# Clearing finished stages' semaphores inside the following stage, in a two-layer graph network kernel

## The chip, the core and the metric

The kernel runs on one core of a Trainium2 chip. The core has five engines with a queue of instructions each: TensorE (PE in the rows; PEld are its weight loads), VectorE (DVE), ScalarE (ACT), GpSimd (POOL) and SyncE (SP). SyncE computes nothing here; it issues most of the transfers. Engines wait for each other by semaphores, counters that one instruction raises and another waits on. The metric is the device time of one execution in microseconds (us); lower is better.

## What is computed

There are 50,000 nodes with 64 features, and 50,000 edges sorted by `dst`. Two layers follow each other, each a layer norm with ReLU, a pass over the edges that sums into nodes, and a residual:

```python
h = relu(layernorm(x));  Wh = h @ W + b
sim = cosine(Wh[src], Wh[dst])                      # layer 0
x = x + scale * (c0 * segment_sum(base * relu(sim) * Wh[dst], src)
               + c1 * segment_sum(-base * relu(-sim) * Wh[dst], src) + c2 * Wh)
h = relu(layernorm(x))                              # layer 1
msgs = mlp(concat(h[dst], h[src]))
agg = segment_sum(msgs, dst)
x = x + mlp(concat(h, agg))
```

## The kernel before

`build` runs six stages in this order. `prepare` loads the edge lists and makes tables. `node_phase0` (tag n0) does layer norm and `Wh` in 49 blocks of 1,024 nodes. `edge_phase` of layer 0 (tag e0) goes through 98 groups of 512 edges: GpSimd gathers rows by index (L1096) and adds results to the table `x1` by index (L1111), and SyncE loads the windows of rows (L1069). `node_phase1` (n1) is the second layer norm, again 49 blocks: SyncE loads `n_x` (L671) and stores `n_h` (L666), and GpSimd also zeroes the table of sums. `edge_phase` of layer 1 (e1) has 98 groups again; TensorE multiplies, VectorE adds into that table (L882). `node_phase2` (n2) is the last MLP over 49 blocks: VectorE copies `agg_sb` beside the rows `n_hs` that SyncE loaded (L1447), TensorE turns them (L1481) and multiplies (L1490).

Each stage is one `Block` or more: every engine runs its own program, and at the Block's end each engine does a DRAIN and then all five meet at a barrier, an EVENT_SEMAPHORE record on each engine in the trace. The records of such an end carry the line of the stage's `Block`: L726 for both edge stages, L648 for n1, L80 for the block that clears. No engine begins the next stage before that barrier. Within a stage each engine's order is a software pipeline written out by `rounds_of_blocks` (L423 is its loop). In the edge stages every engine has two programs, one for graphs whose edges lie near enough together and one for others, and chooses by a value read on the chip (`both_ways`, L733); with these inputs it is the first, and each engine ends it with a jump over the code of the other.

Semaphores are counted up during a stage and have to be zero before their number is used again. The class `Semaphores` keeps a list of those that stages have made. After e0 and again after e1, `give_back` opens a Block of its own in which SyncE clears every semaphore in the list, one instruction each, while the other four engines have nothing in that Block but its barrier; then the numbers are free for the next stages. The first list has 82 semaphores (22 of `prepare`, 31 of n0, 29 of e0), the second 87 (26 of n1, 61 of e1).

At the end of n1 SyncE waits until its stores have landed (L675):

```python
rounds_of_blocks(sp, [(1 - SLOTS, store), (0, load)])
for s in range(SLOTS):
    sp.wait_ge(stored[s], 16 * (ROUNDS + (s == 0)))
```

Of the kernel before, what the change touches and what calls it, by code (L numbers as in the profile page):

```python
# [68 lines left out]
class Semaphores:  # L69
# [5 lines left out]
    def new(self, name):  # L75
        self.made.append(self.ctx.enter_context(self.nc.semaphore(name)))
        return self.made[-1]

    def give_back(self):
        with self.nc.Block() as block:  # L80
            @block.sync
            def _(sp):
                for sem in self.made:
                    sp.sem_clear(sem)
        self.ctx.close()
        self.ctx, self.made = ExitStack(), []


def began(k):

    return not isinstance(k, int) or k > 0


def count(s, k, back=0, slots=0):

    return (slots or SLOTS) * k + s + 1 - back
# [7 lines left out]
def rows_of(tab, base, r=R):  # L104

    return tab[bass.ds(base, P * r), :].rearrange("(p r) d -> p (r d)", r=r)


def build(nc, x, src, dst, edge_weight, edge_weight_n2, W, b, deg_coeff, coeff_param, scale_param,
          mW1, mb1, mW2, mb2, uW1, ub1, uW2, ub2, out):  # L110
    ctx = ExitStack()
    with ctx:
        def sb(name, shape, dt=FP32):
            return ctx.enter_context(nc.sbuf_tensor(name, shape, dt))

        def table(name, shape):
            return nc.dram_tensor(name, shape, FP32, kind="Internal").ap()


        tabs = {name: table(name, [ROWS, D]) for name in ("wh", "x1", "h1", "agg")}  # L120

        tabs["ends"] = table("ends", [2, TILES, P])
        tabs["rel"] = nc.dram_tensor("rel", [TILES, P], FP16, kind="Internal").ap()

        c = dict(
            sems=Semaphores(nc),

            gathered=[[ctx.enter_context(nc.semaphore(f"e{layer}_gathered{s}")) for s in range(ESLOTS)]
                      for layer in range(2)],
            added=[[ctx.enter_context(nc.semaphore(f"e{layer}_added{s}")) for s in range(ESLOTS)]  # L130
                   for layer in range(2)],
            ident=sb("ident", [P, P]),
            not_before=sb("not_before", [P, G * P]),
            near=sb("near", [1, 1], INT32),
            first_i=sb("first_i", [1, TILES], INT32),
            in_window=sb("in_window", [P, WK]),
            in_span=sb("in_span", [P, SPAN], FP16),
            rel_col=sb("rel_col", [P, GROUPS, G]),
            at_i=sb("at_i", [1, TILES], INT32),
            zeros=sb("zeros", [P, SPARE * D]),  # L140
            eps_ln=sb("eps_ln", [P, 1]),
            trash=sb("trash", [P, G]),
            w_blk=sb("w_blk", [P, 2 * D]),
            b_rows=sb("b_rows", [1, R, D]),
            ones_row=sb("ones_row", [1, P]),
            mw1=sb("mw1", [P, DH]), mw1_odd=sb("mw1_odd", [P, DH]), mb1_col=sb("mb1_col", [P, 1]),
            mw2=sb("mw2", [P, D]), mb2_row=sb("mb2_row", [P, D]),
            uw1=sb("uw1", [P, DH]), ub1_col=sb("ub1_col", [P, 1]),
            uw2=sb("uw2", [P, D]), ub2_row=sb("ub2_row", [P, D]),
            mix=sb("mix", [P, 3]),  # L150
            edge_f=sb("edge_f", [P, 3, GROUPS, G]),
            edge_i=sb("edge_i", [P, 2, GROUPS, G], INT32),
            bank=[ctx.enter_context(nc.psum_tensor(f"bank{i}", [P, 512], FP32)) for i in range(8)],
        )
        prepare(nc, c, tabs, src, dst, edge_weight, edge_weight_n2, W, b, deg_coeff, coeff_param,
                scale_param, mW1, mb1, mW2, mb2, uW1, ub1, uW2, ub2)
        node_phase0(nc, c, tabs, x)
        edge_phase(nc, c, tabs, layer=0)
        c["sems"].give_back()
        c["agg"] = sb("agg_sb", [P, NB * D])  # L160
        node_phase1(nc, c, tabs)
        edge_phase(nc, c, tabs, layer=1)
        c["sems"].give_back()
        node_phase2(nc, c, tabs, out)


# [262 lines left out]
def base_of(s, k):  # L429

    if isinstance(k, int) and k * SLOTS + s == BLOCKS - 1:
        return LAST_BASE
    return (k * SLOTS + s) * BLOCK


def rows(a):
    return a.rearrange("p (r d) -> p r d", d=D)
# [205 lines left out]
            rounds_of_blocks(pe, [(-3, turn), (-4, multiply)])  # L643


def node_phase1(nc, c, tabs):

    with ExitStack() as ctx:  # L648
        slots = Slots(nc, c, ctx, "n1")
        h = slots.bufs("h", [P, R * D])  # L650
        ln = LayerNorm(nc, c, slots, [rows(a[:]) for a in h])
        stored = slots.sems("stored")
        agg_clear = slots.sem("agg_clear")
        ln.h_act_ready = slots.sem("h_act_ready")
        SPLIT = R // 2 + 1
        block = ctx.enter_context(nc.Block())

        @block.sync
        def _(sp):
            def store(s, k):  # L660
                sp.wait_ge(ln.h_ready, count(s, k))
                sp.wait_ge(ln.h_act_ready, count(s, k))
                base = base_of(s, k)
                if base is LAST_BASE:
                    sp.wait_ge(stored[SLOTS - 1], 16 * k)
                sp.dma_start(rows_of(tabs["h1"], base), h[s][:]).then_inc(stored[s], 16)  # L666

            def load(s, k):
                if began(k):
                    sp.wait_ge(ln.xc_ready, count(s, k, SLOTS))  # L670
                sp.dma_start(ln.x[s][:], rows_of(tabs["x1"], base_of(s, k))).then_inc(ln.x_in[s], 16)  # L671

            rounds_of_blocks(sp, [(1 - SLOTS, store), (0, load)])
            for s in range(SLOTS):
                sp.wait_ge(stored[s], 16 * (ROUNDS + (s == 0)))  # L675

        @block.vector
        def _(dve):
            def normed(s, k):
                if began(k):  # L680
                    dve.wait_ge(stored[s], 16 * k)
                ln.dve_h_of(dve, s, k, SPLIT)

            rounds_of_blocks(dve, [(0, lambda s, k: ln.dve_total(dve, s, k)), (-3, lambda s, k: ln.dve_rstd(dve, s, k)),
                                   (0, lambda s, k: ln.dve_mean(dve, s, k)),
                                   (-2, lambda s, k: ln.dve_squares(dve, s, k)), (-3, normed)])

        @block.gpsimd
        def _(pool):
            def centre(s, k):  # L690
                pool.wait_ge(ln.mean_ready, count(s, k))
                if began(k):
                    pool.wait_ge(ln.h_ready, count(s, k, SLOTS))
                    pool.wait_ge(ln.h_act_ready, count(s, k, SLOTS))
                nc.gpsimd.tensor_tensor(rows(ln.xc[s][:]), rows(ln.x[s][:]), by_row(ln.mean[s][:]),
                                        ALU.subtract).then_inc(ln.xc_ready, 1)

            def clear(s, k):
                if isinstance(k, int) and k < 2:
                    i, part = k * SLOTS + s, NB * D // (2 * SLOTS)  # L700
                    nc.gpsimd.memset(c["agg"][:, i * part:(i + 1) * part], 0.0).then_inc(agg_clear, 1)

            rounds_of_blocks(pool, [(0, centre), (0, clear)])
            pool.wait_ge(agg_clear, 2 * SLOTS)

        @block.scalar
        def _(act):
            def normed(s, k):
                if began(k):
                    act.wait_ge(stored[s], 16 * k)  # L710
                ln.act_h(act, s, k, range(SPLIT, R))

            rounds_of_blocks(act, [(-2, lambda s, k: ln.act_std(act, s, k)), (0, lambda s, k: ln.act_square(act, s, k)),
                                   (-3, normed)])


def edge_phase(nc, c, tabs, layer):
    with ExitStack() as ctx:
        slots = Slots(nc, c, ctx, f"e{layer}")
        if layer == 0:  # L720
            near = far = EdgeBuffers(c, slots, layer)
        else:
            with ExitStack() as own:
                near = NearBuffers(c, Slots(nc, c, own, f"e{layer}"))
            far = EdgeBuffers(c, slots, layer)
        with nc.Block() as block:  # L726
            edge_programs(nc, block, c, tabs, near, far, layer)


def edge_programs(nc, block, c, tabs, near, far, layer):  # L730
    def both_ways(eng, close, apart):
        is_near = eng.value_load(c["near"][0:1, 0:1], min_val=0, max_val=1)
        with eng.If(is_near > 0):  # L733
# [5 lines left out]
    def _(sp):  # L739
        def apart():  # L740
            edge_loads(nc, sp, c, tabs, far, layer, False)
            if layer == 1:
                for s in range(ESLOTS):
# [4 lines left out]

        both_ways(sp, lambda: edge_loads(nc, sp, c, tabs, near, layer, True) if layer == 0 else near_sync(nc, sp, c, tabs, near),
                  apart)  # L750

    @block.gpsimd
    def _(pool):
# [784 lines left out]
```

## Time and profile before

| | |
|---|---|
| median of 3 runs | 2421.32 us (2419.44 to 2427.26) |
| profiled execution, device time | 2421.7 us |
| its span, first to last instruction | 2419.1 us |
| busy: PE, DVE, ACT, POOL | 1563.3, 1546.1, 864.6, 1689.1 us |
| mean granted TensorE clock | 0.684 of full speed |
| bytes moved | 273.11 MB |

The span is what the trace covers; 2.6 us of the device time lie outside it. No engine is busy over 70% of the span, because the stages have different bounds. Registers, branches, semaphore instructions and the issue of transfers are not counted as busy, so the time that SyncE spends on clearing is in no line of busy time; the queue records, whose engine name ends in q (SPq, DVEq), show it.

How the rows are read. A row of a stretch has its start and end, its length, the busy us of PE, PEld, DVE, ACT and POOL each with the number of instructions, the granted clock (1.00 is full speed), the share of the DMA engines and GB/s. A row of the timeline has start, duration, engine, line, operation and tiles, and in brackets how long the engine had been idle and who released it. A row of records has a line, an engine, an operation, its count, the least, median and greatest duration in ns, and when the first and the last began.

### The profile page before, as it was taken

Reading aid. Unit: us, or ns where it says so; the run is one execution under the profiler, and the core shown is the slowest. Engines: PE = TensorE matmul, PEld = TensorE weight load, DVE = VectorE, ACT = ScalarE, POOL = GpSimd, SP = SyncE. Lnnn points to the kernel's source line nnn. Section 1 sums busy time; section 2 is a strip of 40 time slices with the busy share of each in tenths; the row PEclk is TensorE's granted clock in tenths of the full one; section 3 lists DMA queues with packets and bytes.
Section 4 is the critical chain, followed back from the end, with each engine's and each line's share of the span. In section 5 each row is a group of like instructions: output and inputs, shape, how many; then the busy total and the mean of one; then the engine's idle time right before and its main releaser. Section 6 shows DMA issues by size and latency. Waiting matters only on the chain. (4 is left out here: it accounts for less than half of the span.)

```text
span 2419.1 us, 57388 instructions
## 1 busy us (share of the span) xinstructions
PE 1563.3 (65%) x16004; PEld 1340.3 (55%) x16004; DVE 1546.1 (64%) x5636; ACT 864.6 (36%) x3093; POOL 1689.1 (70%) x1413
## 2 busy tenths in 40 slices
PE   4886755555455454554555540005999999997998
PEld 2555645545455454554554540005999999994454
DVE  5995655555545555555555551894999999994554
ACT  3773322222222222222222221562333333333665
POOL 2775888888888888888888885746777777751322
PEclk6996555555555555555555555557999999998999
DMA  3775544444444444444444422565555555424664
GB/s 99 251 247 172 114 81 84 75 83 82 76 85 80 78 84 74 85 83 75 85 75 83 84 35 15 181 219 150 125 125 124 126 124 126 123 70 119 187 188 145
DMA packets 342562, 273.11 MB, mean 113 GB/s; under 512 B 144834, under 2 KB 273514, under 8 KB 342484
## 3 DMA queue, kind: packets, MB, share of 16 engines
q1 hardware_dynamic: 259028, 233.22, 33.3%
q0 software_dynamic: 81536, 38.61, 15.1%
q8 instruction: 33, 0.54, 0.1%
q10 hardware_dynamic: 1920, 0.37, 0.1%
q14 instruction: 45, 0.37, 0.0%
HBM read 206.69 MB, written 65.34 MB: 112 GB/s over the span
## 5 line engine op out<-in xcount | busy, mean ns | idle before, releaser
L1111 POOL DMA_INDIRECT x<-e_sums,e_to x392 | 622.7, 1588 | 126.1 <-issue 118.6
L1346 PE MATMUL bank<-e_parts,e_same 128*128 128x64 bf16 x2940 | 172.8, 241 | 579.9 <-DVE e_parts L1205 579.9
L1298 PE MATMUL bank<-e_window,e_onehot 128*128 128x64 f32 x2352 | 525.3, 422 | 16.5 <-DMA e_window<-wh 16.5
L1298 PEld LDWEIGHTS bank<-e_window,e_onehot 128*128 128x128 f32 x2352 | 511.8, 332 | 16.9 <-issue 16.8
L1096 POOL DMA_INDIRECT e_ends<-wh,e_ids x392 | 419.1, 1069 | 132.7 <-issue 101.2
L1346 PEld LDWEIGHTS bank<-e_parts,e_same 128*128 128x128 bf16 x2940 | 159.4, 129 | 595.9 <-issue 595.9
L823 POOL DMA_INDIRECT e_near_source<-h,e_near_ids x392 | 394.9, 1007 | 129.0 <-issue 90.2
L1244 ACT ACTIVATE e_sq<-e_ends 128x64 f32<-128x64 f32 x784 | 188.7, 242 | 680.0 <-DMA e_ends<-wh,e_ids 679.9
L1169 DVE SCALAR_TENSOR_TENSOR e_prod<-e_ends 128x64 f32<-128x64 f32 x392 | 65.5, 222 | 363.4 <-DMA e_ends<-wh,e_ids 363.4
L933 PE MATMUL bank<-e_near_to_edge,e_near_window 128*64 128x128 f32 x2352 | 154.5, 282 | 176.3 <-DMA e_near_window<-h 176.3
L933 PEld LDWEIGHTS bank<-e_near_to_edge,e_near_window 128*64 128x64 f32 x2352 | 130.8, 140 | 182.4 <-DVE e_near_to_edge L844 176.7
L1153 DVE SCALAR_TENSOR_TENSOR e_same<-e_owners,e_ef,not_before 128x512 bf16<-128x512 f32 (+3 forms) x392 | 193.3, 549 | 7.3 <-DVE e_ef L1145 4.6
L1415 POOL TENSOR_TENSOR n_x<-n_x,ub_row 128x512 f32<-128x512 f32 x49 | 62.2, 1270 | 183.6 <-DMA n_x<-x 183.6
L906 ACT ACTIVATE e_near_hid<-bank,mb_col 128x512 f32<-128x512 f32 x98 | 67.4, 688 | 330.6 <-PE bank L953 330.6
L882 DVE TENSOR_TENSOR agg_sb<-bank,agg_sb 128x256 f32 x392 | 162.0, 413 | 1.2 <-DVE agg_sb L882 0.6
L977 PEld LDWEIGHTS bank<-e_near_parts,e_near_to_node 128*128 128x128 bf16 x4704 | 150.3, 98 | 17.6 <-DVE e_near_to_node L851 3.9
L977 PE MATMUL bank<-e_near_parts,e_near_to_node 128*128 128x64 bf16 x4704 | 153.2, 193 | 3.6 <-DVE e_near_parts L866 2.6
L1244 ACT ACTIVATION_READ_ACCUMULATOR e_sq<-e_ends 128x1 f32 x784 | 146.1, 186 | 0.0
L1137 DVE TENSOR_SCALAR e_onehot<-e_rel,in_window 128x512 f32<-128x512 f16 x294 | 127.3, 488 | 11.5 <-DMA e_rel<-rel 11.5
L1436 ACT ACTIVATE n_hid<-bank,ub_col 128x512 f32<-128x512 f32 x98 | 103.0, 1154 | 77.9 <-PE bank L1490 77.8
L851 DVE TENSOR_SCALAR e_near_to_node<-in_span,rel_col 128x512 bf16<-128x512 f16 x392 | 127.9, 368 | 0.0
L844 DVE TENSOR_SCALAR e_near_to_edge<-e_near_rel,in_window 128x512 f32<-128x512 f16 x294 | 124.4, 475 | 4.6 <-DMA e_near_rel<-rel 4.6
(150 smaller groups left out, 2857.7 us busy)
## 6 DMA issues: line engine op xcount, KB each, us to landing
e_window<-wh SPq DMA_DIRECT2D x392, 96.0 KB
e_near_window<-h SPq DMA_DIRECT2D x392, 96.0 KB
e_owners<-ends SPq DMA_DIRECT2D x98, 256.0 KB, 3.0
n_x<-x SPq DMA_DIRECT2D x98, 256.0 KB, 3.1
n_x<-in_x_dram SPq DMA_DIRECT2D x49, 256.0 KB, 2.8
wh<-n_wh SPq DMA_DIRECT2D x49, 256.0 KB, 2.0
x<-n_x SPq DMA_DIRECT2D x49, 256.0 KB, 2.3
e_rel<-rel SPq DMA_DIRECT2D x98, 128.0 KB, 3.3
```

What stands on the lines that cost most here:

```text
L823: pool.indirect_dma_start(out=t.source[s][:, j, :], out_offset=None, in_=tabs["h1"], in_offset=bass.IndirectOffsetOnAxis(ap=t.ids[s][:, j: ...
L851: nc.vector.tensor_scalar(t.to_node[s % 2][:, j, :], c["in_span"][:], c["rel_col"][:, bass.ds(ESLOTS * k + s, 1), j:j + 1].rearrange("p a ...
L882: nc.vector.tensor_tensor(here, sums, here, ALU.add).then_inc(t.agg_ready, 1)
L933: last = nc.tensor.matmul(bank[s % 2][half:half + D, j * P:(j + 1) * P], t.window[s][:, j, w, :], t.to_edge[s % 2][:, w, j * P:(j + 1) * P ...
L977: last = nc.tensor.matmul(to[:, at:at + D], t.to_node[s % 2][:, j, b * P:(b + 1) * P], t.parts[s % 2][:, part, j, :], start=part == 0, sto ...
L1096: pool.indirect_dma_start(out=t.ends[s][:, j, at, :], out_offset=None, in_=gathered_tab, in_offset=bass.IndirectOffsetOnAxis(ap=t.ids[s][: ...
L1111: pool.indirect_dma_start(out=added_tab, out_offset=bass.IndirectOffsetOnAxis(ap=t.to[s][:, j:j + 1], axis=0), in_=t.sums[s][:, j, :], in_ ...
L1137: last = nc.vector.tensor_scalar(t.onehot[s][:, w, :], t.rel[s][:], c["in_window"][:, w:w + 1], None, ALU.is_equal)
L1153: nc.vector.scalar_tensor_tensor(t.same[s][:, same_block(j, j):same_block(j, G - 1) + 1, :].rearrange("p b i -> p (b i)"), t.owners[s][:, ...
L1244: nc.scalar.activation(t.sq[s][:, j, end, :], t.ends[s][:, j, end, :], ACT.Square, accum_out=t.norm2[s][:, j, end:end + 1]).then_inc(t.nor ...
L1298: last = nc.tensor.matmul(bank[s % 2][:, j * D:(j + 1) * D], onehot, window, start=w == 0, stop=w == WK - 1)
L1346: last = nc.tensor.matmul(bank[6 + s % 2][:, i * D:(i + 1) * D], t.same[s][:, same_block(j, i), :], t.parts[s][:, part, j, :], start=j == ...
```

## The change

`give_back` no longer opens a Block; it only frees the numbers. A new method `clear` issues the clearing instructions on SyncE, and it is called at two places: in e0, at the end of SyncE's program, for the semaphores of `prepare` and n0; and in n1, after the last store was issued and before the waits for the stores, for the semaphores of e0. The semaphores of n1 and e1 are not cleared any more; n2 gets other numbers, which have been cleared and freed by then.

```diff
+    def clear(self, sp):
+        for sem in self.made:
+            sp.sem_clear(sem)
+
     def give_back(self):
-        with self.nc.Block() as block:
-            @block.sync
-            def _(sp):
-                for sem in self.made:
-                    sp.sem_clear(sem)
         self.ctx.close()
-        self.ctx, self.made = ExitStack(), []
...
         node_phase0(nc, c, tabs, x)
-        edge_phase(nc, c, tabs, layer=0)
-        c["sems"].give_back()
+        first, second = c["sems"], Semaphores(nc)
+        c["sems"] = second
+        edge_phase(nc, c, tabs, layer=0, done=first)
+        first.give_back()
         c["agg"] = sb("agg_sb", [P, NB * D])
-        node_phase1(nc, c, tabs)
+        c["sems"] = Semaphores(nc)
+        node_phase1(nc, c, tabs, done=second)
+        c["sems"] = Semaphores(nc)
         edge_phase(nc, c, tabs, layer=1)
-        c["sems"].give_back()
+        second.give_back()
+        c["sems"] = Semaphores(nc)
         node_phase2(nc, c, tabs, out)
...
             rounds_of_blocks(sp, [(1 - SLOTS, store), (0, load)])
+            done.clear(sp)
             for s in range(SLOTS):
                 sp.wait_ge(stored[s], 16 * (ROUNDS + (s == 0)))
...
         both_ways(sp, lambda: edge_loads(nc, sp, c, tabs, near, layer, True) if layer == 0 else near_sync(nc, sp, c, tabs, near),
                   apart)
+        if done:
+            done.clear(sp)
```

Line numbers differ between the two files (before's L658 is L661 now, L1381 is L1387). The rows of each order list the instructions of SyncE as the program holds them; the clearing instructions are those named ISA at L84 before and at L81 now.

On SyncE at the end of e0 and the start of n1 there stands before, from the end of the edge program to the first loads of n1:

```order
L735 UNCONDITIONAL_BRANCH [waits e0_zeroed]
L81 UNCONDITIONAL_BRANCH [waits barrier_Pool_Activation_PE_DVE_SP_release]
L84 ISA x82
L80 UNCONDITIONAL_BRANCH
L658 UNCONDITIONAL_BRANCH [waits barrier_Pool_Activation_PE_DVE_SP_release]
L671 DMA n_x<-x 128x512 x7
```

and now:

```order
L739 UNCONDITIONAL_BRANCH [waits e0_zeroed]
L81 ISA x53
L730 UNCONDITIONAL_BRANCH
L661 UNCONDITIONAL_BRANCH [waits barrier_Pool_Activation_PE_DVE_SP_release]
L674 DMA n_x<-x 128x512 x7
```

The 82 clears stood between two barriers; 53 of them stand ahead of the only barrier that is left.

On SyncE at the end of n1 there stands before, from its last seven stores to the barrier ahead of e1:

```order
L666 DMA h<-n_h 128x512 [waits n1_h_act_ready,n1_h_ready] x6
L666 DMA h<-n_h 128x512 [waits n1_stored7,n1_h_act_ready,n1_h_ready]
L648 UNCONDITIONAL_BRANCH [waits n1_stored4,n1_stored5,n1_stored3,n1_stored6,n1_stored2,n1_stored7,n1_stored1,n1_stored0]
L738 UNCONDITIONAL_BRANCH [waits barrier_Pool_Activation_PE_DVE_SP_release]
```

and now:

```order
L669 DMA h<-n_h 128x512 [waits n1_h_act_ready,n1_h_ready] x6
L669 DMA h<-n_h 128x512 [waits n1_stored7,n1_h_act_ready,n1_h_ready]
L81 ISA x29
L651 UNCONDITIONAL_BRANCH [waits n1_stored4,n1_stored5,n1_stored3,n1_stored6,n1_stored2,n1_stored7,n1_stored1,n1_stored0]
L742 UNCONDITIONAL_BRANCH [waits barrier_Pool_Activation_PE_DVE_SP_release]
```

The row of 29 clears is new, between the last store and the waits for the stores.

On SyncE at the end of e1 and the start of n2 there stands before:

```order
L735 UNCONDITIONAL_BRANCH [waits e1_numbers_in0]
L81 UNCONDITIONAL_BRANCH [waits barrier_Pool_Activation_PE_DVE_SP_release]
L84 ISA x87
L80 UNCONDITIONAL_BRANCH
L1381 UNCONDITIONAL_BRANCH [waits barrier_Pool_Activation_PE_DVE_SP_release]
L1396 DMA n_hs<-h 128x8x64 x4
```

and now:

```order
L739 UNCONDITIONAL_BRANCH [waits e1_numbers_in0]
L1387 UNCONDITIONAL_BRANCH [waits barrier_Pool_Activation_PE_DVE_SP_release]
L1402 DMA n_hs<-h 128x8x64 x4
```

The 87 clears and one barrier are gone, and nothing stands in their place. On the other four engines the listed rows are the same in both programs, line numbers apart.

## Rows read from the trace of the kernel before

**Rows 1.** Busy time by stretch: n1, e1, n2, and the two strips that clear.

```profile
1511.20:1516.60 5.40, 0.00 (x0) 0.00 (x0) 0.00 (x0) 0.00 (x0) 0.00 (x0) 0.50 0.00 2
1516.60:1644.20 127.60, 0.00 (x0) 0.00 (x0) 116.90 (x245) 80.00 (x245) 72.41 (x65) 0.50 0.61 202
1644.20:2189.00 544.80, 522.46 (x9016) 478.66 (x9016) 479.87 (x1470) 184.03 (x392) 394.87 (x392) 0.98 0.49 119
2189.00:2194.30 5.30, 0.00 (x0) 0.00 (x0) 0.00 (x0) 0.00 (x0) 0.00 (x0) 0.50 0.01 2
2194.30:2419.10 224.80, 210.23 (x980) 106.80 (x980) 113.30 (x196) 128.51 (x147) 62.23 (x49) 0.96 0.60 172
```

**Rows 2.** Records of the clearing line L84, near 1511 and near 2189.

```profile
L84 SPq EVENT_SEMAPHORE_RANGE_CLEAR  x82: 25/30/43, 1511.3 to 1516.4; - x82
...
L84 SPq EVENT_SEMAPHORE_RANGE_CLEAR  x87: 25/25/35, 2189.1 to 2194.0; - x87
```

**Rows 3.** Barrier and drain records at both places (lines L726 and L80).

```profile
L726 POOLq DRAIN  x1: 5555/5555/5555, 1505.4 to 1505.4; - x1
L726 SPq EVENT_SEMAPHORE  x1: 17/17/17, 1511.2 to 1511.2; - x1
...
L80 SPq EVENT_SEMAPHORE  x1: 17/17/17, 1516.6 to 1516.6; - x1
...
L726 SPq EVENT_SEMAPHORE  x1: 17/17/17, 2189.0 to 2189.0; - x1
...
L80 SPq EVENT_SEMAPHORE  x1: 17/17/17, 2194.3 to 2194.3; - x1
```

**Rows 4.** Timeline and records of SyncE's queue, end of its program in e0.

```profile
1400.26 3.65 SPq L1069 DMA_DIRECT2D e_window<-wh  x4
...
L726 SPq DRAIN  x1: 7/7/7, 1404.1 to 1404.1; - x1
```

**Rows 5.** Timeline and records of SyncE's queue, end of n1.

```profile
1641.88 0.33 SPq L666 DMA_DIRECT2D h<-n_h  x1
...
DMA to landing us min/median/max: 2.0/2.0/3.2
...
L675 SPq EVENT_SEMAPHORE  x4: 17/28/28, 1642.3 to 1642.4; - x4
...
L648 SPq COMPARE_BRANCH  x1: 38/38/38, 1643.9 to 1643.9; - x1
```

**Rows 6.** Timeline at the start of n1.

```profile
1516.72 3.19 SPq L671 DMA_DIRECT2D n_x<-x  x7
1519.43 0.69 DVE L479 TENSOR_REDUCE n_total<-n_x 128x8 f32<-128x512 f32 x1 [46.99 <-DMA n_x<-x]
```

**Rows 7.** Timeline and records around the end of e1 and the start of n2.

```profile
2185.42 0.98 DVE L882 TENSOR_TENSOR agg_sb<-bank,agg_sb 128x256 f32 x2 [0.20 <-DVE agg_sb L882]
...
L726 DVEq DRAIN  x1: 76/76/76, 2188.8 to 2188.8; - x1
...
2194.38 0.76 DVE L1447 COPY n_hs<-agg_sb 128x512 f32<-128x512 f32 x2 [7.99 <-PEq L80]
...
2197.95 1.94 PE L1481 MATMUL bank<-ident,n_hs 128*128 128x128 f32 x8 [14.17 <-DMA n_hs<-h]
```

**Rows 8.** The chain that ended last, its first long piece in n2.

```profile
2194.34 3.48 DMA n_hs<-h
```

**Rows 9.** Busy time and granted clock in short stretches of e1 and n2.

```profile
1663.00:1670.00 7.00, 3.58 (x44) 2.78 (x44) 1.78 (x6) 1.16 (x2) 5.45 (x6) 0.98 0.67 188
1670.00:1674.00 4.00, 4.00 (x32) 3.00 (x30) 0.95 (x3) 1.16 (x2) 3.09 (x4) 0.57 0.39 93
...
2198.00:2206.00 8.00, 7.12 (x21) 4.58 (x22) 2.05 (x4) 1.17 (x2) 2.81 (x3) 0.50 1.01 219
2206.00:2210.00 4.00, 4.00 (x20) 1.95 (x19) 0.90 (x2) 3.72 (x5) 1.00 (x1) 1.00 0.00 0
```

**Rows 10.** Durations of line L1490's matmuls, ns least/median/most.

```profile
L1490 PE MATMUL bank<-n_hsT,uw x196: 592/592/1062, 2202.5 to 2405.9; 128*128 128x512 f32 x196
```

More of the change, by code:

```diff
@@ L643, in _, with node_phase1 @@
             rounds_of_blocks(pe, [(-3, turn), (-4, multiply)])
-def node_phase1(nc, c, tabs):
+def node_phase1(nc, c, tabs, done):
     with ExitStack() as ctx:
@@ L714, in _, with edge_phase @@
                                    (-3, normed)])
-def edge_phase(nc, c, tabs, layer):
+def edge_phase(nc, c, tabs, layer, done=None):
     with ExitStack() as ctx:
@@ L726, in edge_phase, with edge_programs @@
         with nc.Block() as block:
-            edge_programs(nc, block, c, tabs, near, far, layer)
-def edge_programs(nc, block, c, tabs, near, far, layer):
+            edge_programs(nc, block, c, tabs, near, far, layer, done)
+def edge_programs(nc, block, c, tabs, near, far, layer, done):
     def both_ways(eng, close, apart):
```

## Prediction

> **What bounds the kernel now.** I cut the span at the barriers first. Two strips between stages, 5.4 us and 5.3 us long, have 0.00 us of work on all five engines and 2 GB/s of transfers [rows 1]. Everything waits there, whatever bounds the stages. The records of the clearing line fill them: 82 clears begin between 1511.3 and 1516.4, 87 between 2189.1 and 2194.0 [rows 2]. One clear takes 25 to 43 ns, but they begin 5.1 / 81 = 63 ns apart in the first strip and 4.9 / 86 = 57 ns in the second, so it is SyncE's pace that counts. Around them stand two barriers each: the one that ends the edge stage at 1511.2 and 2189.0, the one that ends the clearing at 1516.6 and 2194.3 [rows 3].
>
> Next, who waits behind the second barrier of each pair. In n1 VectorE's first reduction starts 2.7 us after SyncE's first load, which goes out 0.1 us after the barrier [rows 3, 6]. In n2 the chain that ended last begins with the first load of `n_hs`, issued at 2194.34 and landed 3.48 us later [rows 8], and TensorE's first instruction follows at 2197.95, released by it [rows 7]. Both stages start with loads that SyncE can issue only after the barrier. So each strip lies on the path of the whole kernel, and a microsecond off it is a microsecond off the end.
>
> **The change part by part.** *Removed:* from the edge stage's barrier to the clearing barrier, 1516.6 - 1511.2 = 5.4 us and 2194.3 - 2189.0 = 5.3 us [rows 3]. This holds the clears, the second drain and the second barrier. Sum 10.7 us. What precedes stays: GpSimd's drain of 5.555 us ahead of the first barrier [rows 3] and VectorE's way from its last addition, which ends at 2185.42 + 0.98 = 2186.40, to its drain at 2188.8 [rows 7].
>
> *Added in e0:* 53 clears at 63 ns, 3.3 us of SyncE. Nothing is queued behind them but SyncE's own drain and barrier. SyncE's last window load was issued by 1400.26 + 3.65 = 1403.91, it drains at 1404.1 [rows 4] and then waits for the barrier of 1511.2 [rows 3], 107 us. The cover is what the other engines have still to do for the groups already loaded, and GpSimd's last indexed additions. Cost nothing; without this cover 3.3 us.
>
> *Added in n1:* 29 clears between the last store and the waits for the stores, at 57 to 63 ns, 1.7 to 1.8 us. The barrier into e1 waits behind them. The cover is the landing of that last store: issued 1641.88 to 1642.21, landing 2.0 us after 1641.88, and SyncE's branch goes at 1643.9 [rows 5]. The clears end at 1642.21 + 1.8 = 1644.0. The waits for the stores, of which the records show four within 0.2 us [rows 5], come after that now and not under the landing, so the branch goes at about 1644.2 instead of 1643.9. Cost 0.3 us; with no cover it would be 1.8 us, and with the faster pace 0.1 us.
>
> *Removed at n2:* the third place gets nothing for the 87 clears. There the gain is whole.
>
> *Numbers and code.* Semaphores get other numbers and the four computing engines lose an empty Block. No row prices a number; the order of their instructions is the same, so I cost it at nothing. What could follow a shorter strip are two things, and both have rows.
>
> First, code. Each engine ends its edge program with a jump over the other program. VectorE is 2188.8 - 2186.40 = 2.4 us on its way from its last addition to its drain [rows 7]; I read most of this as the fetch of code that the jump leads to. If another such stall comes right after, the strip covered it before. Bounds: nothing, since in n2 VectorE's copy begins 0.04 us after SyncE's load and TensorE starts only 3.6 us later [rows 7, 8], so even a stall of 2.4 us would be hidden there, as it would under the 2.7 us of n1 [rows 6]; and 2.4 us at each place if it falls on SyncE. SyncE left its jump in e0 107 us earlier, and it drains 0.2 us after its last load [rows 4]. I take nothing.
>
> The Trainium skill, page "Runtime: NRT & Kernel Launch", section "Instruction fetch mechanics", says that a taken branch whose target is not in the engine's current two pages of code forces a fetch before it can go on. The trace agrees as far as the 2.4 us of VectorE go. By that rule the four other engines, which used the strip to read on, could stall after the barrier; this is the second rival, and it speaks against this change.
>
> Second, the clock. TensorE is idle for 14.17 us ahead of n2 [rows 7]; it will be 8.9 us. The strip has clock 0.50 already [rows 1], the lower level of 1.2 GHz, and stays so till 2206.0, 8 us after TensorE began again [rows 9]. A matmul of n2 takes up to 1062 ns there against 592 ns at 2.4 GHz [rows 10], a factor of 1.79. Had all 8 us been at the higher clock, they would be 8 x (1 - 1/1.79) = 3.5 us less; twice as long a stretch costs the same 3.5 us more. In e1 the clock dipped once more after its first rise, to a mean of 0.57 over 4 us [rows 9]; that dip absent or there twice is 1.8 us either way. I take nothing for both, and keep plus and minus 5 us as bounds.
>
> *Sum.* -5.4 - 5.3 + 0 + 0.3 = -10.4 us. Against the profiled execution of 2421.7 us (span 2419.1 and 2.6 us outside it, which no edit touches) this gives 2411.3 us; this execution is 0.4 us over the median of the runs, so the same sum on the median gives 2411 us, 0.43% less.
>
> **The rivals.**
> 1. *A clear stays on the path.* If SyncE paces n1's end more than I think, all 1.8 us show: gain 8.9 us, 2412.4 us. That the change did not do what it says would need SyncE last at the end of e0 too, which 107 us speak against.
> 2. *A fetch stall takes the strip's place,* by the rule above, on the path once or twice at 2.4 us: 2413.3 or 2415.7 us. For it: the strip is where engines could read on. Against it: loads in flight for 2.7 and 3.5 us cover the computing engines.
> 3. *The clock takes it back.* TensorE's restarts in e1 and n2 fall differently against the clock's changes: up to 5 us, 2416 us. The same mechanism the other way gives 2406 us.
> 4. *Slower.* The clock stays at 1.2 GHz in e1 after a later start. TensorE is busy 522 of 544.8 us there [rows 1], so each us of its work at the higher clock becomes up to 1.79 us. To end 7.3 us above the present time it has to lose 17.7 us, that is 17.7 / 0.79 = 22 us of e1's work at the lower clock beyond today's. Speaking against it, the mean clock over all of e1 is 0.98 [rows 1], and TensorE is as busy as before. 2429 us.
>
> **How the numbers follow.** What a measurement of this kernel can tell from no change is 0.3%, 7.3 us, so the bound of "faster" is 2414.0 us. Forecast as summed: 0.70, own range 2407 to 2415, of which 0.66 is faster. Rival 1: 0.03, faster. Rival 2: 0.08, of which 0.05 faster. Rival 3 as a loss: 0.12, of which 0.04 faster, since a small part of the 5 us leaves the gain above 7.3. As a further gain: 0.05, faster. Rival 4: 0.02. Faster 0.83, same 0.15, slower 0.02. The gain is sure in the trace, but it is only 1.4 times the bound, and the three runs of before lie 7.8 us apart. The range is 2405 to 2417 us: the forecast less 5 us of clock and 1 us of runs below, rival 3 and twice rival 2 above.
>
> **What would show it.** In the trace of after: no strip without work, the first load of n1 within 0.1 us of the only barrier, the same in n2. 53 clears begin at about 1404 and end by 1408, a hundred us ahead of the barrier. 29 clears end near 1.8 us after the last store's issue, and SyncE's branch follows 0.3 us later than it did, counted from that issue. VectorE's first copy in n2 follows the barrier by under 0.1 us; if it follows by 2 us, there is the fetch stall, and if TensorE's first instruction then comes more than 3.7 us after the barrier, it costs. TensorE's low-clock stretch in n2 stays near 8 us. The prediction is wrong if GpSimd's drain of 5.555 us before the first barrier grows, if e0, the longest stage and untouched, runs otherwise, or if the stages after the barriers take longer than 127.6 + 0.3 and 224.8 us [rows 1].

## The result, and the profile after

The changed kernel takes 2414.24 us (median of 6 runs, 2411.05 to 2418.68) against 2426.51 us for the kernel before (6 runs, 2419.44 to 2427.81). The ratio is 0.9958 with a 95% interval of 0.9941 to 0.9974: 10.2 us less, between 6.3 and 14.3 (the two medians lie 12.3 us apart, inside this interval). Ratios here and below are taken over the runs within 1.5% of the fastest of the same kernel, which in this section is all of them. The prediction had 10.4 us less.

The profiled execution of the changed kernel took 2418.68 us with a span of 2416.6 us, only 2.5 us under the span of before. So the two traces don't show the gain as one number; cut at the barriers they do. These are its stretches from barrier to barrier, in the columns of [rows 1]: e0, n1, e1, n2.

```profile
204.30:1518.00 1313.70, 679.90 (x5292) 663.71 (x5292) 681.44 (x3430) 350.30 (x2058) 1048.55 (x784) 0.50 0.44 79
1518.00:1646.20 128.20, 0.00 (x0) 0.00 (x0) 116.95 (x245) 80.00 (x245) 72.41 (x65) 0.50 0.60 201
1646.20:2193.00 546.80, 523.25 (x9016) 479.38 (x9016) 486.74 (x1470) 183.90 (x392) 394.77 (x392) 0.98 0.48 118
2193.00:2416.60 223.60, 209.18 (x980) 106.44 (x980) 113.81 (x196) 128.45 (x147) 62.24 (x49) 0.97 0.61 173
```

There is no strip left: each stretch begins where the one ahead of it ends. Against [rows 1] the strips give -5.4 and -5.3 us, n1 is 0.6 us longer, e1 2.0 us longer, n2 1.2 us shorter. e0, whose end stood at the barrier of 1511.2 [rows 3], ends at 1518.0, 6.8 us later. Together that is the 2.5 us. The 6.8 us of e0 do not come from the clears: SyncE's last loads in e0 were issued at 1407.02, where it was 1400.26 before [rows 4], so the whole delay was there before the first clear began. I take it for drift. The order of the other engines' instructions in e0 is the same, and in the experiments below e0's end moves by twice as much between traces of the same e0.

Next the records of the clears and barriers in the changed kernel (L81 clears, L730 ends the edge stages, L679 waits for the stores of n1, L651 ends n1), which answer to [rows 2 to 5]; ahead of them the timeline rows of SyncE's last loads in e0 and last store in n1.

```profile
1407.02 3.64 SPq L1075 DMA_DIRECT2D e_window<-wh  x4
...
L81 SPq EVENT_SEMAPHORE_RANGE_CLEAR  x53: 25/30/43, 1410.9 to 1414.0; - x53
...
L730 SPq DRAIN  x1: 129/129/129, 1414.4 to 1414.4; - x1
...
L730 SPq EVENT_SEMAPHORE  x1: 17/17/17, 1518.0 to 1518.0; - x1
...
1643.13 0.33 SPq L669 DMA_DIRECT2D h<-n_h  x1
...
L81 SPq EVENT_SEMAPHORE_RANGE_CLEAR  x29: 25/30/37, 1643.5 to 1645.5; - x29
...
L679 SPq EVENT_SEMAPHORE  x4: 17/28/28, 1645.6 to 1645.8; - x4
...
L651 SPq COMPARE_BRANCH  x1: 43/43/43, 1645.9 to 1645.9; - x1
L651 SPq DRAIN  x1: 7/7/7, 1646.0 to 1646.0; - x1
L651 SPq EVENT_SEMAPHORE  x1: 17/17/17, 1646.2 to 1646.2; - x1
```

In e0 the 53 clears begin 0.2 us after SyncE's last loads were issued, take 3.1 us (60 ns each), and SyncE then waits 104 us for the barrier. In n1 the 29 clears stand between the last store and the waits for the stores. They take 2.0 us, 71 ns from one to the next, and the waits behind them pass in 0.3 us, so the store, issued at 1643.13, had landed by the time they were reached. From the issue of the last store to the barrier it is 3.1 us, where it was 2.3 us [rows 5, and the stretch's end in rows 1].

At the start of n2 (records of L730 and the timeline) there is something that [rows 7] don't have:

```profile
L730 SPq EVENT_SEMAPHORE  x1: 17/17/17, 2193.0 to 2193.0; - x1
...
L730 PEldq EVENT_SEMAPHORE  x1: 51/51/51, 2193.0 to 2193.0; - x1
L730 DVEq EVENT_SEMAPHORE  x1: 21/21/21, 2195.1 to 2195.1; - x1
...
2193.05 2.96 SPq L1402 DMA_DIRECT2D n_hs<-h  x4
2195.19 0.76 DVE L1453 COPY n_hs<-agg_sb 128x512 f32<-128x512 f32 x2 [4.83 <-DVEq L730]
...
2196.43 1.94 PE L1487 MATMUL bank<-ident,n_hs 128*128 128x128 f32 x8 [8.69 <-DMA n_hs<-h]
```

The other engines leave the barrier at 2193.0, VectorE 2.1 us later. Its first copy is late by as much. TensorE doesn't feel it: it was released by the load of `n_hs`, and its first instruction starts 3.4 us after the barrier, where it started 3.65 us after it before [rows 3, 7].

The clock (stretches of the changed kernel, in e1 and n2):

```profile
1666.50:1670.00 3.50, 3.50 (x20) 2.34 (x20) 1.18 (x3) 0.65 (x2) 2.82 (x3) 0.51 0.71 176
...
1676.60:1683.40 6.80, 6.33 (x36) 5.17 (x38) 1.39 (x5) 1.46 (x3) 4.97 (x7) 0.51 0.39 92
...
2196.00:2202.00 6.00, 4.69 (x18) 3.83 (x19) 1.80 (x4) 1.17 (x2) 0.83 (x1) 0.50 1.25 256
...
2202.30:2206.00 3.70, 3.70 (x15) 1.78 (x13) 1.12 (x2) 2.38 (x3) 2.70 (x3) 0.98 0.31 80
```

Early in e1 the clock fell to 1.2 GHz twice, for about 3.5 and 6.8 us, where it fell once for under 4 us before [rows 9]; in n2 it was back at 2.4 GHz 5.9 us after TensorE began, where it took 8 us. By the prediction's factor of 1.79 the 6.9 us more at the lower clock in e1 would cost 3.0 us and the 2.1 us less in n2 give back 0.9, both estimates. That goes with the 2.0 us that e1 lost and the 1.2 us that n2 gained; I did not separate it from other drift in e1.

### The profile page after: what moved, and what is told of

The parts are those of the page before. It is cut to its first block and busy times, and to the rows that moved or that the text cites. A ratio compares the mean times of both kernels' runs of the same rounds, so it can differ in the third digit from the quotient of the medians.

```text
span 2416.6 us, 57279 instructions
## 1 busy us (share of the span) xinstructions
PE 1562.8 (65%) x16004; PEld 1340.6 (55%) x16004; DVE 1553.3 (64%) x5636; ACT 864.0 (36%) x3093; POOL 1695.9 (70%) x1413
## 5 line engine op out<-in xcount | busy, mean ns | idle before, releaser
L1102 POOL DMA_INDIRECT e_ends<-wh,e_ids x392 | 425.2, 1085 | 132.8 <-issue 102.1
## 6 DMA issues: line engine op xcount, KB each, us to landing
e_rel<-rel SPq DMA_DIRECT2D x98, 128.0 KB, 3.2
```

The lines of the kernel that those rows point to most:

```text
L1102: pool.indirect_dma_start(out=t.ends[s][:, j, at, :], out_offset=None, in_=gathered_tab, in_offset=bass.IndirectOffsetOnAxis(ap=t.ids[s][: ...
```

## The experiments

Twelve runs on three chips. On all three this kernel, before the change too, takes about 2830 us and not 2425, and the runs of one kernel can lie 60 to 70 us apart; the last section shows where. So ratios of the whole time say little here, and their intervals are too narrow for this scatter. What is read is lengths between barriers in the traces: on these chips n1 and n2 are as long as on the first within 1.0 us, and e1 is not. Ratios and intervals are given all the same.

### The changed kernel again, twice

> The changed kernel once more, beside the three variants. Both theories: 10 us less than before, ratio 0.9958. In the profile the vector engine should again leave the barrier into the last stage about 2.1 us after the others, if that is a fetch of code at a fixed place in its program; at another time or not at all, if it was chance.

> The changed kernel on the same chip as the three others, so that they can be compared. Theory: 10.1 us less than before, ratio 0.9958 where e1 takes 545 us; n1 128.2 us, the vector engine 2.1 us late at the last barrier but one, TensorE's first instruction 3.4 to 3.5 us after it.

Ratios 0.9964 (0.9918 to 1.0009) and 0.9984 (0.9935 to 1.0033). The plain means of all runs are 2820.2 us for 12 runs against 2832.0 for 35, and 2819.4 against 2829.9, with standard errors of 3 to 5 us each: 11.8 and 10.4 us less, in line with the sum, but neither clear of no change alone. In the traces n1 is 128.3 us long in both, and VectorE is late by 2.2 and 2.1 us at the same barrier. Of the second run, the records of L730 at the end of e1:

```profile
L730 DVEq DRAIN  x1: 76/76/76, 2611.9 to 2611.9; - x1
L730 SPq EVENT_SEMAPHORE  x1: 17/17/17, 2612.1 to 2612.1; - x1
...
L730 DVEq EVENT_SEMAPHORE  x1: 21/21/21, 2614.2 to 2614.2; - x1
```

So the late exit is a property of the program and not chance. It costs nothing: the eight traces in which VectorE leaves the barrier into n2 late (2.1 to 2.6 us) have an n2 of 223.5 to 224.4 us, the six in which it is on time, or 0.3 us late, one of 224.1 to 225.4.

### Only the first strip taken away, twice

```diff
+    def clear_apart(self):
+        with self.nc.Block() as block:
+            @block.sync
+            def _(sp):
+                self.clear(sp)
...
         node_phase1(nc, c, tabs, done=second)
-        c["sems"] = Semaphores(nc)
         edge_phase(nc, c, tabs, layer=1)
+        c["sems"].clear_apart()
+        c["sems"].give_back()
         second.give_back()
```

> The changed kernel, but the semaphores of n1 and e1 are cleared in a Block of their own ahead of n2, as before. Theory (each strip is on the path by its full length): 5.4 - 0.3 = 5.1 us less than before, 2421 us for a before of 2426, and a strip of 5.3 us in the trace at the end of e1. Rival (only one of the strips mattered): either all 10 us are still gained, or none.

> Only the strip after e0 taken away, once more, on another chip if it is one where e1 takes 545 us. Theory: 5 us less than before, ratio 0.998, half of the changed kernel's gain; strip of 5.3 us at the end of e1, in which the vector engine leaves the first barrier 2.1 us late as in the changed kernel, since its code up to there is the same. Rival: that lateness was chance and is absent.

Ratios 0.9996 (0.9950 to 1.0042) and 1.0001 (0.9958 to 1.0045); these can't tell 5 us from none, and neither can the plain means, 5.7 and 3.7 us less with standard errors of 4 to 6. The time therefore does not show that this kernel gains half; the trace shows that one strip is gone and the other there, from 2606.4 to 2611.4 in the first run, 5.0 us where 5.3 were expected. n1 is 128.1 and 128.8 us. The records at the end of e1 in the first run (L737 ends the edge stage, L84 the clearing):

```profile
L737 SPq EVENT_SEMAPHORE  x1: 17/17/17, 2606.4 to 2606.4; - x1
...
L737 DVEq EVENT_SEMAPHORE  x1: 21/21/21, 2608.5 to 2608.5; - x1
...
L84 SPq EVENT_SEMAPHORE  x1: 17/17/17, 2611.4 to 2611.4; - x1
L84 DVEq EVENT_SEMAPHORE  x1: 21/21/21, 2611.4 to 2611.4; - x1
```

VectorE leaves the first barrier 2.1 us late here too, inside the strip, and is on time at the second. This kernel has the strip of before at this place and lacks only the Block after e0. In the kernel before, VectorE left this same barrier on time:

```profile
L726 SPq EVENT_SEMAPHORE  x1: 17/17/17, 2189.0 to 2189.0; - x1
...
L726 DVEq EVENT_SEMAPHORE  x1: 21/21/21, 2189.1 to 2189.1; - x1
```

What makes it late is therefore not the missing strip beside it. What differs ahead of this barrier is that its program is shorter by the Block after e0, so the late exit goes with where its code stands. That it is a fetch of code is my reading and not shown.

### Empty Blocks in place of the strips

```diff
+def empty_block(nc):
+    with nc.Block() as block:
+        @block.sync
+        def _(sp):
+            pass
...
+        empty_block(nc)
         first.give_back()
...
+        empty_block(nc)
         second.give_back()
```

> The changed kernel with an empty Block after e0 and after e1: the second barrier is back, the clears are not. Theory A (the clears are the price, a barrier alone costs 0.2 us): two strips of 0.2 to 0.3 us, 0.5 us more than the changed kernel, not to be told from it by time. Theory B (the vector engine reaches the code after its jump late, by a fetch of 2.1 us, which the 5.3 us of clears had hidden): the second strip is 2 to 2.4 us long, since every engine now waits at the second barrier for the vector engine, and the first is 0.2 to 0.3 us.

Ratio 0.9997 (0.9953 to 1.0040). The records of the second place (L739 ends the edge stage, L88 the empty Block):

```profile
L739 SPq EVENT_SEMAPHORE  x1: 17/17/17, 2584.7 to 2584.7; - x1
L739 DVEq EVENT_SEMAPHORE  x1: 21/21/21, 2584.7 to 2584.7; - x1
...
L88 SPq EVENT_SEMAPHORE  x1: 17/17/17, 2585.0 to 2585.0; - x1
L88 DVEq EVENT_SEMAPHORE  x1: 21/21/21, 2585.0 to 2585.0; - x1
```

A Block with nothing in it costs 0.3 us, at the first place too (1517.6 to 1517.9). Theory A holds: of 5.3 us, 5.0 are the clears. Theory B fails, and for an instructive reason: with the Block after e0 back, VectorE's program ahead of this barrier is as before, and it is on time.

### Every clear ten times, in the strips of the kernel before

```diff
             def _(sp):
-                for sem in self.made:
-                    sp.sem_clear(sem)
+                for _ in range(10):
+                    for sem in self.made:
+                        sp.sem_clear(sem)
```

> The kernel before, with every semaphore cleared ten times in the two Blocks (820 and 870 clears). Theory (a clear costs SyncE's pace of 57 to 63 ns, and the strips are on the path): 738 x 0.063 + 783 x 0.057 = 91 us more than before, strips of 51.6 and 49.6 us. Rival (most of a strip is its barriers, or starting up): clearly less than 91 us.

Ratio 1.0372 (1.0221 to 1.0523), 2939.45 us (2 runs) against 2843.01, 96 us more; the interval reaches from 63 to 149 us. The strips:

```profile
L727 SPq EVENT_SEMAPHORE  x2: 17/17/17, 1515.4 to 2655.0; - x2
...
L80 SPq EVENT_SEMAPHORE  x2: 17/17/17, 1565.4 to 2707.3; - x2
```

They are 50.0 and 52.3 us long, 91.6 us more than the 10.7 of before; 61 and 60 ns a clear. n1 and n2 are 127.7 and 225.4 us long, so they absorb none of it, and the time grew by as much as the strips within its interval: the strips are on the path by their whole length, and their length goes with the number of clears.

### The clears of e0's end twenty and forty times

```diff
         if done:
-            done.clear(sp)
+            for _ in range(20):          # 40 in the second
+                done.clear(sp)
```

> The changed kernel with the 53 clears at the end of SyncE's program in e0 done twenty times, 1060 clears, 67 us. Theory (a cover of 104 us from the end of SyncE's loads to the barrier): no more than the changed kernel, SyncE drains at about 1475. Rival (clears disturb the other engines' semaphores while they work): e0's last groups take longer, and the time grows by some part of 67 us.

> The same with forty times, 2120 clears, 134 us at 63 ns. Theory: the cover of 107 us from the end of SyncE's loads to the barrier is used up, and the rest, 134 - 107 = 27 us, shows. Rival (the clears are free as long as other engines work, whatever their number, or cost all of their time): 0 us or 134 us.

Twenty times: ratio 0.9897 (0.9849 to 0.9946), which would be 29 us of gain for a kernel that can't gain more than the changed one's 10, so nothing is read from it. SyncE drained at 1509.7, not at 1475, and the barrier stood at 1513.7, within the spread of the other traces; hidden, but only just. Forty times: ratio 1.0230 (1.0073 to 1.0387, 2 runs), and the barrier stood at 1574.2. GpSimd began its drain at 1507.8; in the other traces the barrier follows that by 5.7 to 5.8 us, so about 60.6 us show and not 27. The second kernel's drains and barriers (GpSimd's and SyncE's, the first of each two at the end of e0), and its clears, counted in stretches of 5 us, the first while GpSimd's indexed transfers run, the second after them:

```profile
L730 POOLq DRAIN  x2: 5559/7692/9826, 1507.8 to 2616.0; - x2
...
L730 SPq EVENT_SEMAPHORE  x2: 17/17/17, 1574.2 to 2665.0; - x2
...
L81 SPq EVENT_SEMAPHORE_RANGE_CLEAR  x28: 3/18/711, 1442.2 to 1447.0; - x28
...
L81 SPq EVENT_SEMAPHORE_RANGE_CLEAR  x81: 25/30/37, 1510.0 to 1515.0; - x81
```

28 clears in 5 us with one of 711 ns there, 81 here. Over the covered part 1060 clears took 102 us in the first kernel, 97 ns each; in the second they ran 60 ns apart once the transfers were over. So the cover is what the theory says, and the pace under it was mis-sized: the clears neither cost all their time nor none. The rival of the first kernel, that clears disturb the others, isn't borne out by a barrier at 1513.7.

### The clears of n1 ten times

```diff
-            done.clear(sp)
+            for _ in range(10):
+                done.clear(sp)
             for s in range(SLOTS):
                 sp.wait_ge(stored[s], 16 * (ROUNDS + (s == 0)))
```

> The changed kernel with the 29 clears in n1 done ten times, 290 clears, 17 to 18 us. Theory (the cover there is the landing of the last store, 1.7 us): 15.7 to 16.5 us more than the changed kernel, all of it in n1. Rival (stores of the last blocks give more cover than the one landing): less.

Ratio 1.0019 (0.9960 to 1.0078). The records of the barriers ahead of n1 and at its end:

```profile
L731 SPq EVENT_SEMAPHORE  x1: 17/17/17, 1521.5 to 1521.5; - x1
...
L651 SPq EVENT_SEMAPHORE  x1: 17/17/17, 1665.7 to 1665.7; - x1
```

n1 is 144.2 us long, 16.0 us over the changed kernel's 128.2, as expected: the 261 clears more cost 61 ns each. So the cover at this place is used up by the first 29, which fits the landing of the last store.

### The clears of e0's semaphores in e1 instead of n1, twice

```diff
             rounds_of_blocks(sp, [(1 - SLOTS, store), (0, load)])
-            done.clear(sp)
...
-        node_phase1(nc, c, tabs, done=second)
+        node_phase1(nc, c, tabs)
         c["sems"] = Semaphores(nc)
-        edge_phase(nc, c, tabs, layer=1)
+        edge_phase(nc, c, tabs, layer=1, done=second)
```

> The changed kernel, but the 29 semaphores of e0 are cleared at the end of SyncE's program in e1 instead of in n1. Theory: SyncE is idle there for over 40 us, so the clears cost nothing, and n1 is 0.3 to 0.6 us shorter than in the changed kernel (127.6 us as before). Rival (n1's extra is drift and not the clears): n1 stays at 128.2 us. The time as a whole will not tell them apart, n1's length in the trace will.

> The clears of e0's semaphores at the end of SyncE's program in e1, once more. Theory: n1 is 127.6 us from barrier to barrier, 0.6 us less than in the changed kernel; ratio to before 0.9956, at best 0.0003 better than the changed kernel and not to be told from it. Rival (n1's length drifts by itself): 128.2 us again.

Ratios 0.9945 (0.9886 to 1.0004) and 0.9928 (0.9864 to 0.9991), which by their intervals don't differ from the changed kernel's beside them. The barriers around n1 in the first trace, and its 29 clears in e1:

```profile
L729 SPq EVENT_SEMAPHORE  x2: 17/17/17, 1509.9 to 2581.9; - x2
...
L651 SPq EVENT_SEMAPHORE  x1: 17/17/17, 1637.5 to 1637.5; - x1
...
L81 SPq EVENT_SEMAPHORE_RANGE_CLEAR  x29: 3/14/700, 2527.7 to 2536.8; - x29
```

n1 is 127.6 us in both traces (1509.9 to 1637.5 and 1519.0 to 1646.6), as it is in the two traces of before's n1 (127.6 and 127.7); the nine traces with the 29 clears once in n1 give 128.0 to 128.8. The clears end 45 us ahead of the barrier of 2581.9. So the clears are what makes n1 longer, by 0.4 to 1.2 us and by 0.6 in the first trace, and this version is the better one by as much; only the stage's length shows it, not the time.

### The two programs of an edge stage in the other order

```diff
-        with eng.If(is_near > 0):
-            close()
-        with eng.Else():
-            apart()
+        with eng.If(is_near < 1):
+            apart()
+        with eng.Else():
+            close()
```

> The changed kernel with the two programs of each edge stage in the other order in the code: the one that runs stands last, so no engine jumps over the other's code at its end, but every engine jumps over it at its start. Theory (the 2.4 us between the vector engine's last addition and its drain are a fetch of code after that jump, and so is its late exit from the barrier): the gap at the end of e1 falls to 0.1 us, the gap from GpSimd's last landing to its drain at the end of e0 likewise, and both edge stages begin up to 2.4 us later; the time stays within 3 us of the changed kernel. Rival (the gap is the vector engine finishing its last addition, or the drain itself): the gap stays 2.4 us.

Ratio 0.9987 (0.9947 to 1.0028). The end of e1 and start of n2 in its timeline, with the barrier's records and TensorE's first matmul of e1:

```profile
2609.57 0.98 DVE L888 TENSOR_TENSOR agg_sb<-bank,agg_sb 128x256 f32 x2 [0.20 <-DVE agg_sb L888]
2611.18 0.76 DVE L1453 COPY n_hs<-agg_sb 128x512 f32<-128x512 f32 x2 [0.62 <-DVEq L730]
...
L730 SPq EVENT_SEMAPHORE  x1: 17/17/17, 2610.8 to 2610.8; - x1
...
L730 DVEq EVENT_SEMAPHORE  x1: 21/21/21, 2611.1 to 2611.1; - x1
...
1660.63 2.83 PE L939 MATMUL bank<-e_near_to_edge,e_near_window 128*64 128x128 f32 x24 [170.69 <-DMA e_near_window<-h]
```

The copy and the first matmul in the changed kernel on the same chip (after_c):

```profile
2614.30 0.76 DVE L1453 COPY n_hs<-agg_sb 128x512 f32<-128x512 f32 x2 [5.11 <-DVEq L730]
...
1653.74 2.83 PE L939 MATMUL bank<-e_near_to_edge,e_near_window 128*64 128x128 f32 x24 [171.22 <-DMA e_near_window<-h]
```

VectorE's last addition ends at 2610.55 and the barrier opens at 2610.8. In the changed kernel beside it VectorE was idle for 5.11 us between addition and copy, here for 0.62. Of the 4.5 us of difference 2.65 lie ahead of the barrier, and 1.8 are the late exit, which is down from 2.1 to 0.3. At the end of e0 GpSimd's drain begins 3.5 us after its last transfer was issued (1514.99 to 1518.5) and not 5.8 (1507.82 to 1513.6). The start of e1 pays for it: TensorE's first matmul comes 8.2 us after the barrier (1652.4 to 1660.63) and not 6.0 (1647.7 to 1653.74). This bears out the theory: the 2.4 us are the jump over the other program's code, and a jump costs about as much wherever it stands. The DMA view of the traces shows what goes on in that time. It has queues named "instruction", with transfers of 8 and 16 KB; which engine each one serves it doesn't say. Two of them fall into the 2.7 us between VectorE's last addition and its drain in the changed kernel, and two in the kernel before; with the programs swapped there is none between the last addition and the barrier, but seven between the barrier into e1 and TensorE's first matmul, where the changed kernel has none. For the late exit the same view settles nothing: one such transfer follows that barrier by 0.3 us in the first trace of the changed kernel, and by 0.4 us with the empty Blocks, where VectorE is on time.

## Why the prediction was right

**The strips lie on the path by their whole length.** Right: they are gone, and ten times the clears made them 91.6 us longer and the kernel 96 us slower. Predicted 5.4 and 5.3 us. The empty Blocks split them into 5.1 and 5.0 us of clears and 0.3 us of barrier each.

**e0's 53 clears cost nothing.** Right: they end 104 us ahead of the barrier. On the chips of the experiments this cover holds a good 1060 clears, not the 1700 that 63 ns would give.

**n1's 29 clears cost 0.3 us.** The mechanism was right and the term mis-sized: 0.6 us in the first trace, 0.4 to 1.2 over all. They came 71 ns apart and not 57 to 63, and the step from the last store's issue to the barrier went from 2.3 to 3.1 us, 0.8 us, of which n1's length shows 0.6. Moving the clears took all of it away.

**A shorter strip brings no stall.** The step that is only half right. The fetch stall of the second rival is there, 2.1 us on VectorE, and hidden, as that rival's "against" said, under the 3.4 us until TensorE gets its rows. But I had it as something that the strip covered before. It was not there before: taking away the Block after e0 moved VectorE's code, and in the kernel that keeps the second strip VectorE is late within it. That the jump itself costs 2.4 us was shown by the swapped programs. That the late exit is a fetch too rests only on its coming in all ten traces without the Block after e0, the swapped one apart, and in neither of the two of before nor with the empty Blocks; its cause stays open.

The Trainium skill, page "Runtime: NRT & Kernel Launch", section "Instruction fetch mechanics", has a taken branch out of the two pages at hand force a fetch. The traces agree as far as the jump goes: with the code jumped over standing first, the way from VectorE's last addition to the barrier is 2.65 us shorter and that from the barrier to TensorE's first matmul 2.2 us longer, and the transfers of the instruction queues move with it. How far the jump reaches in the code was not measured.

**The clock.** Bounded at 5 us either way; the profiled pair shows 2.0 us more in e1 and 1.2 less in n2. The stretch at the lower clock in n2, which was to stay near 8 us, took 5.9.

**The sum.** -10.7 + 0.6 = -10.1 us from the stages' lengths, -10.4 predicted, -10.2 measured by the ratio. The times can't tell these three apart, their interval being 8 us wide; that the sum is right rests on the stages. The forecast of 2411 us as a time had some luck in it to come within 3.2 us: it was reckoned from a median of 2421.3 us, and with three more runs the kernel before has 2426.5. Two of the signs of being wrong came about: e0 ran 6.8 us longer, and n1 took 128.2 us where 127.9 were allowed. GpSimd's drain did not grow (5.560 us), and n2 stayed under 224.8 us. The rest of the difference between the two profiled executions is e0. Its end stands at 1511.2 and 1515.4 us in the two traces with the code of before, and between 1507.8 and 1521.5 in the nine that have the clears once at its end and the programs in their old order; the spread of a stage that nobody changed is larger than the gain.

## What to carry to other kernels

Cut a trace at its barriers and look for strips in which no engine is busy: busy-time tables don't list what fills them, and here, where the next stage began with loads that had to wait for the barrier, they were on the path by their whole length. Work of an engine that only issues can go to the end of its program in a long stage, ahead of the barrier where it waits anyway; put it where it waits for other engines (e0, e1) and not where it is itself the last (n1). And a gain of this size is read from the lengths of stages; one pair of profiled executions showed 2.5 us of 10.

## What was not expected of the hardware

**Chips differ by 400 us in one stage.** The stage e1 is 964 us long in the second of the two repeats of the changed kernel, and 547 in its first trace. Its n1 and n2 are as long as in the first trace within 0.6 us (128.3 and 224.2 us). The cost groups of TensorE in the middle of e1, of that repeat and then of the kernel before (line, mean ns, idle time ahead of it and who ended it), over 700 and 300 us:

```profile
L983 PE MATMUL bank<-e_near_parts,e_near_to_node 128*128 128x64 bf16 x3494 | 160.6, 199 | 134.1 <-issue 132.9 <-DVE e_near_to_edge L850 1.0
```

```profile
L977 PE MATMUL bank<-e_near_parts,e_near_to_node 128*128 128x64 bf16 x2736 | 89.1, 193 | 0.0
```

On the slower chip the mean length of one of these matmuls is about the same, 199 ns against 193, but 134 us of idle time stand before them, and for 133 of them the trace shows nothing that TensorE waited for. The granted clock is lower too, 0.80 over the stage against 0.98. All three chips of the experiments were so: e1 took 938 to 981 us in their twelve traces. What makes TensorE wait was not found.

**On those chips single instructions of SyncE take up to 0.7 us while the edge stages run.** The 1060 clears in e0 came 97 ns apart on the average against 60, and single ones took up to 718 ns. On the chip of the first trace the 53 clears in e0 took 25 to 43 ns each and 3.1 us in all; on a slower chip the same 53 (first repeat of the changed kernel) took up to 576 ns each and 4.0 us. It is not a matter of clears: in e1 of both repeats the branches of SyncE's loop (L426) take up to 703 and 702 ns, against 50 in the first trace. Nor does the number of clears in a row do it, since the 820 and 870 of the lengthened strips, on such a chip too, took 25 to 43 ns each. What else is different there, the indexed transfers or the other engines' work, was not separated.

**GpSimd's drain after its indexed transfers** takes 5.5 us at the end of e0 (5.555 us in [rows 3], 5.560 after the change), with all other engines at the barrier. What it waits for, and whether it can be shortened, was not tried.
